# Attention pooling: the score and sum stretches of two chunks put together

## What is computed

```python
h = relu(einsum('bse,eh->bsh', behavior_emb, W_b) + (candidate_emb @ W_c)[:, None, :] + fc1_b)
scores = einsum('bsh,h->bs', h, fc2_w[:, 0]) + fc2_b[0]
attn = softmax(scores, axis=-1)
user_interest = einsum('bse,bs->be', behavior_emb, attn)
x = concatenate([user_interest, candidate_emb], axis=1)
logit = (relu(x @ mlp1_w + mlp1_b) @ mlp2_w + mlp2_b)[:, 0]
```

## Time and profile before

| what | value |
|---|---|
| time, median of 3 runs | 266.76 us (266.63 to 266.91) |
| time of the profiled execution | 266.47 us |
| its span, first to last instruction | 264.7 us |
| TensorE busy, matmuls | 259.3 us (98%) |
| VectorE busy | 224.2 us (85%) |
| ScalarE busy | 200.6 us (76%) |
| GpSimd busy | 29.4 us (11%) |
| moved by DMA | 105.87 MB, mean 400 GB/s over the span |
| granted TensorE clock | full (2.4 GHz) throughout |

### The profile page before, as it was taken

How to read it: one execution, slowest core, us unless ns; L and a number is a source line. 1 busy time by engine, 2 the same in 40 slices (tenths; PEclk the granted TensorE clock), 3 DMA queues, 4 the chain that set the end, 5 groups by cost and what they waited for, 6 DMA issues and landing times.

```text
span 264.7 us, 10384 instructions
## 1 busy us (share of the span) xinstructions
PE 259.3 (98%) x3942; PEld 212.4 (80%) x3942; DVE 224.2 (85%) x397; ACT 200.6 (76%) x481; POOL 29.4 (11%) x38
## 2 busy tenths in 40 slices
PE   8999999999999999999999999999999999999995
PEld 7557788888888868888888888888888888888973
...
GB/s 247 430 433 422 422 426 420 424 424 420 426 422 423 426 420 429 429 426 426 424 429 429 426 426 426 428 428 422 428 429 428 426 426 426 429 428 426 391 32 0
DMA packets 10544, 105.87 MB, mean 400 GB/s; under 512 B 1184, under 2 KB 1696, under 8 KB 2592
## 3 DMA queue, kind: packets, MB, share of 16 engines
...
q10 hardware_dynamic: 288, 0.20, 0.2%
...
## 4 chain that ended last, share of the span: by engine, by line
PE 60%; DMA 18%; DVE 14%; issue 4%; ACT 1%; DVEq 1%; POOL 0%; ACTq 0%; SPq 0%; POOLq 0%
DMA xt<-in_behavior_t 18%; PE s_ps L632 12%; PE u_ps L643 11%; PE z_ps L617 10%; PE z_ps L613 9%; DVE xl L454 9%; PE z_ps L614 8%; DVE hidden L464 5%; PE z_ps L608 4%; PE z_ps L750 2%; PE z_ps L643 1%; ACT xh L329 1%; PE z_ps L684 1%; PE z_ps L727 1%; PE z_ps L721 1%
## 5 line engine op out<-in xcount | busy, mean ns | idle before, releaser
L454 DVE TENSOR_TENSOR xl<-xt,xh 128x800 fp32r<-128x800 f32 x120 | 123.2, 1047 | 8.9 <-ACT xh L329 8.7
L329 ACT CAST xh<-xt 128x800 fp32r<-128x800 f32 x120 | 100.4, 862 | 34.2 <-DMA xt<-in_behavior_t 33.1
L371 ACT ACTIVATE hidden<-z_ps,bias 128x200 f32<-128x200 f32 x256 | 88.3, 428 | 7.4 <-PE z_ps L608 3.6
L613 PE MATMUL z_ps<-xh,w_hi 128*128 128x512 f32 x240 | 86.4, 360 | 0.5 <-DVE hidden L464 0.5
L614 PE MATMUL z_ps<-xh,w_lo 128*128 128x512 f32 x240 | 79.4, 345 | 0.0
L464 DVE TENSOR_TENSOR hidden<-z_ps,neg_bias 128x800 f32<-128x800 f32 x64 | 62.9, 982 | 3.3 <-PE z_ps L608 2.0
L617 PE MATMUL z_ps<-xl,w_hi 128*128 128x512 f32 x240 | 64.8, 351 | 0.9 <-DVE xl L454 0.2
L613 PEld LDWEIGHTS z_ps<-xh,w_hi 128*128 128x128 f32 x240 | 45.0, 188 | 16.3 <-issue 6.0
L299 POOL TENSOR_TENSOR weights_by_row<-weights,masks_sb 128x400 f32<-128x400 f32 x31 | 27.6, 890 | 218.3 <-ACT weights L336 177.3
L632 PE MATMUL s_ps<-hidden,f_col 128*3 128x160 f32 (+4 forms) x1280 | 50.1, 301 | 0.0
L614 PEld LDWEIGHTS z_ps<-xh,w_lo 128*128 128x128 f32 x240 | 45.1, 188 | 5.6
...
## 6 DMA issues: line engine op xcount, KB each, us to landing
...
later_sb<-in_later SPq DMA_DIRECT2D x1, 258.5 KB, 19.6
...
```

The source lines that it names most:

```text
L329: nc.scalar.copy(xh[g][:, :], xt[q][:, g, :]).then_inc(xh_made, 1)
L371: op = nc.scalar.activation(hidden[q % 2][:, g, :, mine], z[:, :, mine], ACT.Relu, bias=bias[:, bass.ds(c * ROWS + g * EACH + b, 1)])
L454: nc.vector.tensor_tensor(xl[g][:, :], xt[q][:, g, :], xh[g][:, :].bitcast(F32), ALU.subtract).then_inc(xl_made, 1)
L613: nc.tensor.matmul(z[:, a:b], w_hi[:, :], xh[g][:, a:b], start=True, stop=False)
```

## The change

- The stretch comes in even periods alone (and once in period 31). In period c (even) it holds the scores of chunks c-2 and c-1 and then the weighted sums of chunks c-4 and c-3. Odd periods are four groups in a row.
- `hidden` becomes ten buffers of one group each: groups 0 and 1 of an even chunk have two buffers in turn, the other six groups of a pair of chunks one. `scores` holds two chunks side by side.
- The softmax of two chunks is seven instructions in place of twelve: the transposition of 320 columns, a maximum per chunk, and two `exp_bias`. Each counts 2 on its semaphore.
- ScalarE and VectorE have other orders in even and odd periods, and `Z_SHORT`, the table from which `Z_SLOTS` comes, has other entries.
- SyncE issues `xt` of two chunks, then `x` of two chunks; `later` is loaded behind the last `xt`; the last `x` comes in two pieces, and TensorE's last weighted sum waits for the first piece before its first 13 tiles.
- At the end, `mlp_candidates`, `row_sums(1)`, `mlp_pooled` of part 0 and `spread_inverses(1)` go ahead of the weighted sum of chunk 31, and `logits(0)` goes right behind it. ScalarE's part-0 relus go ahead of the last copies. VectorE masks the last weights in one instruction.

```diff
-Z_SHORT = (6, 14)
+Z_SHORT = (3, 11)
...
-LAG = 3
...
-        hidden = [sb(f"hidden{i}", [P, GROUPS, TILES, Q]) for i in range(2)]
-
-        scores = [sb(f"scores{i}", [P, RUN * Q]) for i in range(2)]
+
+        hidden_first = [[sb(f"hidden_first{i}_{g}", [P, TILES, Q]) for g in range(2)] for i in range(2)]
+        hidden_rest = [sb(f"hidden_rest{i}", [P, TILES, Q]) for i in range(2 * GROUPS - 2)]
+
+        scores = sb("scores", [P, 2, RUN * Q])
...
-                with eng.Fori(0, (CHUNKS - FIRST - 1) // X_BUFS) as turn:
+                with eng.Fori(0, (CHUNKS - FIRST - 2) // X_BUFS) as turn:
                     for j in range(FIRST, FIRST + X_BUFS):
                         body(turn * X_BUFS + j, j % X_BUFS, FIRST)
+                body(LAST - 1, (LAST - 1) % X_BUFS, FIRST)
...
+        def hidden_of(q, g):
+
+            if q % 2 == 0 and g < 2:
+                return hidden_first[q // 2][g]
+            return hidden_rest[g - 2 if q % 2 == 0 else g + 2]
...
+            load_transposed(X_BUFS, 0)
             load(0, None)
+            load(1, None)
+            for c in (X_BUFS + 1, X_BUFS + 2):
+                load_transposed(c, c - X_BUFS)
+            load(2, None)
+            load(3, None)
+            with sp.Fori(0, CHUNKS // X_BUFS - 2) as turn:
+                for j in (0, 2):
+                    c = turn * X_BUFS + (2 * X_BUFS - 1 + j)
+                    load_transposed(c, (X_BUFS - 1 + j) % X_BUFS)
+                    load_transposed(c + 1, j)
+                    load(c - 3, j)
+                    load(c - 2, j + 1)
+            load_transposed(LAST, LAST % X_BUFS)
             sp.dma_start(later_sb[:, :], later).then_inc(later_loaded, 16)
-            for c in range(X_BUFS, 2 * X_BUFS):
-                load_transposed(c, c - X_BUFS)
-                load(c - LAG, None if c - LAG < X_BUFS else c - LAG - X_BUFS)
-            with sp.Fori(0, CHUNKS // X_BUFS - 2) as turn:
-                for j in range(X_BUFS):
-                    c = turn * X_BUFS + (2 * X_BUFS + j)
-                    load_transposed(c, j)
-                    load(c - LAG, (j - LAG) % X_BUFS)
-            for c in range(CHUNKS - LAG, CHUNKS):
+            for c in range(CHUNKS - X_BUFS, LAST):
                 load(c, c % X_BUFS)
+            sp.wait_ge(pooled_done, CHUNKS - X_BUFS)
+            cols = LAST_RUN * E
+            sp.dma_start(x[LAST % X_BUFS][:, 0:cols], behavior_v[LAST, :, 0:cols]).then_inc(x_half, 16)
+            sp.dma_start(x[LAST % X_BUFS][:, cols:], behavior_v[LAST, :, cols:]).then_inc(x_loaded[LAST % X_BUFS], 16)
...
+                if phase == LAST:
+                    high_half(c, q, 3, None, False)
+                    biased_relu(c, q, 1, phase)
+                    exponents(c - 1, (q + 1) % 2, IN_PAIRS + 2 * ALONE_STEPS, False)
+                    biased_relu(c, q, 3, phase)
+                    return
+                if phase > 1:
+                    high_half(c, q, 3, None, phase == WHOLE)
+                if q % 2 == 1:
+                    next_half(0)
+                    biased_relu(c, q, 1, phase)
+                    next_half(1)
+                    biased_relu(c, q, 3, phase)
+                    next_half(2)
+                    return
                 biased_relu(c, q, 1, phase)
                 next_half(0)
                 next_half(1)
-                if phase == 1:
-                    exponents(0, 0, True)
-                if flush:
-                    copy_pooled4(c - LAG, u_ps)
-                if phase == 1:
-                    biased_relu(c, q, 3, phase)
-                    next_half(2)
-                else:
-                    exponents(c - 1, (q + 1) % 2, phase <= 2)
-                    next_half(2)
-                    biased_relu(c, q, 3, phase)
-                next_half(3)
+
+                for n in range(2):
+                    exponents(c - 2 + n, n, pair_steps(c - 2) + 2 * (PAIR_STEPS - 1 + n), phase == 2)
+                if phase > 2:
+                    copy_pooled4(c - X_BUFS + 1, u_ps)
+                next_half(2)
+                biased_relu(c, q, 3, phase)
 
...
-            exponents(LAST, LAST % 2, False)
+            exponents(LAST, LAST % 2, IN_PAIRS + 4 * ALONE_STEPS, False)
+            relu(0)
+            relu(1)
             copy_pooled4(LAST, last_pair_ps)
             copy_pooled_t(LAST, last_pair_ps[:, P:P + 2 * ROWS])
-            relu(0)
-            relu(1)
...
                 if step == 0:
-                    dve.wait_ge(scores_done, c + 1)
+                    dve.wait_ge(scores_done, c + n)
                     if not early:
 
-                        dve.wait_ge(weights_made, c - 1)
-                    op = nc.vector.transpose(scores[buf][:, :], s_ps[:, 0:RUN * Q])
+                        dve.wait_ge(weights_made, c if buf is None else c - buf)
+                    if buf is None:
+                        op = nc.vector.transpose(scores[:, :, :].rearrange("p c t -> p (c t)"), s_ps[:, 0:2 * RUN * Q])
+                    else:
+                        op = nc.vector.transpose(scores[:, buf, :], s_ps[:, buf * RUN * Q:(buf + 1) * RUN * Q])
                 else:
...
+                biased_max(c, q, 0, phase)
+                if phase == LAST:
+                    low_half(c, q, 3)
+                    for n in range(ALONE_STEPS):
+                        softmax(c - 1, 0, n, IN_PAIRS, False)
+                    biased_max(c, q, 2, phase)
+                    return
+                if q % 2 == 1:
+                    if phase > 1:
+                        low_half(c, q, 3)
+                    next_low(0)
+                    biased_max(c, q, 2, phase)
+                    next_low(1)
+                    return
+                low_half(c, q, 2)
+                low_half(c, q, 3)
+                if phase == 2:
                     shifts()
                     dve.wait_ge(shift_step, 3)
-                else:
-                    if phase == 2:
-                        low_half(c, q, 2)
-                    low_half(c, q, 3)
-                for n in range(SOFTMAX_STEPS):
-                    softmax(c - 1, (q + 1) % 2, n, phase <= 2)
-                if phase == 1:
-                    biased_max(c, q, 2, True)
-                    next_low(0)
-                    next_low(1)
-                    return
+                for n in range(PAIR_STEPS):
+                    softmax(c - 2, None, n, pair_steps(c - 2), phase == 2)
                 next_low(0)
-                biased_max(c, q, 2, False)
                 next_low(1)
+                biased_max(c, q, 2, phase)
                 next_low(2)
...
-            for n in range(SOFTMAX_STEPS):
-                softmax(LAST, LAST % 2, n, False)
-            mask_last(0)
-            mask_last(1)
+            for n in range(ALONE_STEPS):
+                softmax(LAST, 1, n, IN_PAIRS + 2 * ALONE_STEPS, False)
+            normalise(0)
...
+            add_out_bias(0)
             normalise(1)
             last_relu(0)
             last_relu(1)
-            for part in range(2):
...
+            add_out_bias(1)
...
-                pe.wait_ge(x_loaded[q], loads(c, q))
                 if q % 2 == 0:
+                    pe.wait_ge(x_loaded[q], loads(c, q))
 
                     pe.wait_ge(relu_made, LAST * HALF + 1)
                     pe.wait_ge(masked, c + 1)
                     sum_tiles(c, q, last_pair_ps, 0, WHOLE_TILES, GROUPS - 1).then_inc(pooled_done, 1)
                 else:
+                    pe.wait_ge(x_half, 16)
                     pe.wait_ge(last_masked, 1)
                     sum_tiles(c, q, last_pair_ps, 0, LAST_RUN, None)
-                    pe.wait_ge(last_masked, 2)
+                    pe.wait_ge(x_loaded[q], loads(c, q))
                     sum_tiles(c, q, last_pair_ps, LAST_RUN, WHOLE_TILES, LAST_RUN).then_inc(pooled_done, 1)
...
-                    if g == PHASE_AT and phase > LAG + 1 and (q - LAG) % 2 == 0:
-                        transpose_sums(c - LAG - 1, beside_z(q, g))
-                    if g == PHASE_AT and phase >= 1:
-                        score(c - 1, (q + 1) % 2, phase == 1)
-                    if g == PHASE_AT and phase >= LAG:
-                        weighted_sum(c - LAG, (q - LAG) % X_BUFS, phase == LAG)
+                    if g != PHASE_AT or phase < 2:
+                        continue
+                    if phase == LAST:
+                        transpose_sums(LAST - X_BUFS, beside_z(q, g))
+                        score(LAST - 1, (q - 1) % X_BUFS, pair_steps(LAST - 3) + 2)
+                        weighted_sum(LAST - 3, (q - 3) % X_BUFS, False)
+                    elif q % 2 == 0:
+                        if phase == 2:
+                            shift_sums()
+                            pe.wait_ge(f2_col_made, 2)
+                        if phase == FIRST:
+                            transpose_sums(c - X_BUFS - 1, beside_z(q, g))
```

(24 more changed lines are left out.)

129 lines of the change are left out of this document (66 added, 63 removed).

## The result

The changed kernel takes **271.54 us** (271.28 to 271.89, 4 runs) against 266.74 us for the kernel before on the same chip: ratio 1.018, 95% interval 1.0163 to 1.0198, so 4.8 us slower. The forecast was 267.1 us, and 271.5 lies outside its range. The profiled execution took 271.89 us with a span of 270.1 us (264.7 before).

What follows compares the result with a forecast made beforehand. Loads were taken to bound the body, so its terms cost nothing; at the end, span 264.7 + 1.1 - 0.3 - 0.45 = 265.05, + 0.35 to 0.4 us on the run, giving 267.1 us. Range 265.3 to 269.0 us.

Steps and rivals of the forecast that it cites:

- What bounds the kernel now: Body of the kernel before: loads set the pace, 15.38 us per two chunks, with TensorE fitting under it by a hair.
- Part 1: Every second stretch removed: 0.57 us each, about 8.6 us off TensorE, costed at nothing in the load-paced body.
- Part 2: Body under the new order: stretch ends 0.1 us after `xt` lands; without load waits 14.94 us a pair against 15.38.
- Part 3: Loads issued in pairs: same bytes, no cost; last `xt` lands at 238.2 us, last byte still at 254.0.
- Part 4: Kernel's end: stretch 0.3 us earlier, last relu 1.1 later, 0.3 and 0.45 won back; + 0.35 to 0.4 us.
- The rivals: Alternatives: end slack 265.3 (0.23), TensorE pace 261 (0.03), ScalarE's loop 271 (0.12), bigger end bubbles 268.4 (0.20), unremoved idle 267.1.
- ScalarE's loop: Body: ScalarE's chain of copy and relus becomes the pace, 14 pairs costing 4 us: 271 us; chance 0.12.

Runs made afterwards that it cites:

- light loads: The kernel before, loading only the first 128 columns of `x` for chunks 4 to 31: 261.34 us in one run.
- the split kernel: The changed kernel with the two weighted sums moved behind tile 3 of the same even period, ScalarE's copy of the sums behind its relu of tile 3: 266.9 us, ratio 1.002.
- one experiment: The changed kernel with its two weighted sums behind tile 2 instead of tile 1, ScalarE's copy where it stood: 271.38 us, ratio 1.0195.

## Why the prediction was wrong

**What bounds the kernel now: right.** The loads paced the kernel before; with light loads it runs 15.01 us a pair in place of 15.38.

**Part 1: the step that failed.** "Since the loads pace the body, I cost this at nothing there" counted only what the merged stretch saves. It has a price that I didn't look for: 384 instructions at 15 ns, run for the first time under full DMA engines, outrun the packets that bring them. A packet is 256 of them, 3.8 us of work, and the next takes 5.4 to 5.6 us to come. Four waits, 1.59 + 1.78 + 1.68 + 1.91 = 6.96 us from start to start (6.0 of it counted as idle matmuls), 5.05 of them ahead of period 10. The saving was mis-sized too, 0.57 us for a stretch less: measured 0.21 (5.67 against 5.88). The idle times that I added up were those of the weight loads, while matmuls were still at work: TensorE's matmuls were busy 31.92 of 32 us.

**Part 2: the pace right, the cover wrong.** The loop without waits for loads was worked out at 14.94 us a pair; it is 15.03. ScalarE's list holds, and so does the wait for its relu, 0.22 us a pair where I looked for half a microsecond. But the forecast let the body be at the loads' heels at once, so that nothing which delays TensorE would show. In fact it gains on the loads by no more than 15.38 - 15.03 = 0.35 us a pair. In the split kernel, without the waits, the scores of period 30 start at 231.35, 1.4 us ahead of the forecast (238.3 - 5.54, some 232.8). In the change they start at 236.19, 3.4 us behind it: the 5.05 us of waits ahead of period 10, less that lead and 0.2 us by which the split kernel's last pair was slower; nothing else of them was made good, since without the waits the pace is the same 15.03. The 1.91 us in period 30 come on top. 3.4 + 1.9 = 5.3 us, and 265.05 + 5.3 = 270.35, against the span of 270.1.

**Part 3: right in the main.** DMA share 1.00 to 1.01 and 422 to 428 GB/s in every stretch from 24 to 248 us; the last bytes landed at 253.97 us, forecast 254.0. The last `xt` landed at 236.85, 1.35 us sooner than the 238.2 forecast, which changed nothing, as TensorE was 7 us behind it. No load was what TensorE waited for in the body.

**Part 4: right.** From the last sum's start to the end 6.66 us, forecast 6.65; alone in the kernel before + 0.5 us, forecast + 0.35 to 0.4 (ratio 1.0023).

**The rivals.** None held this. The slower rival nearest in time, ScalarE's loop at 271, would have shown pairs of over 15.4 us; they are 15.03. It came true in one experiment, where ScalarE's copy waited 1.1 us longer and a pair took 15.37 us, so the mechanism exists; the change just doesn't reach it. The Trainium skill (TensorEngine Tiling (Array Packing), Key Properties) states that a change of tiling mode drains TensorE, and gives no time for it. In these traces it is small, 0.21 us for a stretch less, and it did not decide anything: the loop with one stretch a pair and that with two run at 15.03 and 15.01.
